# Two attention blocks and a mixture of experts on one core: first maxima, one transfer a row, expert weights by slices, lists in pieces

## The reference

```python
# block 1, per image, xf: [128, 1024]
f = softmax((theta_w @ xf).T @ (phi_w @ xf) / 8)        # 64 embedded channels
x = x + proj_w @ (f @ xf.T).T
t = tokens of x                                          # [4, 1024, 128]
# block 2
z = layernorm(t)
t = t + softmax((z Wq + bq)(z Wk + bk).T / sqrt(128)) (z Wv + bv)
# block 3: each token goes to 2 of 8 experts
z = layernorm(t)
top_w, top_i = top_k(z Wg + bg, 2);  w = softmax(top_w)
t = t + sum over both of w * (gelu(z W1[e] + b1[e]) W2[e] + b2[e])   # hidden size 512
```

## Time and profile before

| | us |
|---|---|
| median of three runs | 489.34 |
| the profiled execution | 489.35 |
| its span | 487.6 |
| TensorE busy | 389.0 (80%) |
| DVE busy | 370.3 (76%) |
| ACT busy | 335.2 (69%) |
| POOL busy | 313.0 (64%) |

### The profile page before, as it was taken

The page is one execution under the profiler, slowest core; times in us unless marked ns, Lnnn a source line. Parts: engine busy times, 40 slices in busy tenths (PEclk is TensorE's granted clock), DMA queues, the critical chain, the costliest instruction groups (busy, mean ns, idle before and its releaser), DMA issues.

```text
span 487.6 us, 12633 instructions
## 1 busy us (share of the span) xinstructions
PE 389.0 (80%) x3948; PEld 291.9 (60%) x3949; DVE 370.3 (76%) x1012; ACT 335.2 (69%) x636; POOL 313.0 (64%) x309
## 2 busy tenths in 40 slices
PE   2666669999988799989987876658989999999552
PEld 1433337666665466666655644646879898989321
DVE  2577989998897787889898588667976666666863
ACT  3635887778785499876756875558778787888320
POOL 9200132755699856598857857767777777777780
PEclk9988999999998999999999989778999999999955
DMA  6750000610000000000510101133355333334717
GB/s 216 169 93 0 1 0 3 151 25 3 1 1 0 2 1 1 1 1 2 137 38 12 31 27 40 51 88 94 91 127 132 105 101 93 98 94 113 225 49 258
DMA packets 43836, 32.62 MB, mean 67 GB/s; under 512 B 17686, under 2 KB 36905, under 8 KB 43785
## 3 DMA queue, kind: packets, MB, share of 16 engines
q1 hardware_dynamic: 39242, 22.59, 19.0%
q0 software_dynamic: 4544, 9.38, 5.8%
HBM read 18.33 MB, written 13.60 MB: 65 GB/s over the span
## 4 chain that ended last, share of the span: by engine, by line
PE 41%; DVE 31%; ACT 10%; issue 8%; POOL 6%; DMA 2%; SPq 1%; ACTq 0%; POOLq 0%; DVEq 0%
PE MX L696 13%; PE PV L696 11%; PE SC L696 11%; DVE mx L1519 6%; DVE EL L1542 5%; PE PR L696 4%; POOL ybuf L685 3%; ACT EH L1168 2%; ACT E L1167 2%; ACT QK L1076 2%; DVE QK L1493 2%; DVE EH L1738 1%; ACT X L1076 1%; PE PR L965 1%; DVE TOK L1561 1%
## 5 line engine op out<-in xcount | busy, mean ns | idle before, releaser
L1167 ACT ACTIVATE E<-SC 128x512 f32<-128x512 f32 x128 | 77.2, 603 | 43.4 <-PE SC L696 36.5
L696 PE MATMUL PV<-VH,EH 128*128 128x129 f16 x512 | 96.0, 227 | 3.0 <-DVE TOK L1561 3.0
L696 PE MATMUL SC<-QK 128*128 128x512 f16 x320 | 90.6, 389 | 8.2 <-ACT EH L1168 6.1
L618 POOL TENSOR_TENSOR EL<-E,EH 128x1024 f32 (+1 forms) x28 | 59.6, 2128 | 56.7 <-ACT EH L1168 56.7
L696 PE MATMUL PV<-VH,EL 128*128 128x129 f16 x512 | 95.6, 225 | 0.0
L696 PE MATMUL PV<-VL,EH 128*128 128x128 f16 x512 | 95.6, 223 | 0.0
L1519 DVE TENSOR_REDUCE mx<-MX 128x1 f32<-128x1024 f32 x64 | 78.0, 1219 | 18.8 <-PE MX L696 18.5
L685 POOL DMA_INDIRECT ybuf<-EL,yid x62 | 70.0, 1130 | 18.9 <-issue 17.4
L569 POOL DMA_INDIRECT zbuf<-ZZ,posi x64 | 66.4, 1038 | 21.3 <-issue 18.2
L1168 ACT ACTIVATE EH<-SC 128x512 f32 (+1 forms) x128 | 77.6, 606 | 0.0
L696 PE MATMUL MX<-QK,EH 128*128 x624 | 62.2, 246 | 1.9 <-DVE EL L1749 1.9
(11 more groups left out here) (231 smaller groups left out, 886.8 us busy)
## 6 DMA issues: line engine op xcount, KB each, us to landing
EH<-zbuf SPq DMA_DIRECT2D x39, 130.0 KB, 2.4
X<-in_x_dram SPq DMA_DIRECT2D x4, 512.0 KB, 5.1
zbuf<-zer SPq DMA_DIRECT2D x16, 128.0 KB, 4.0
X<-in_L_ffn_W_dram SPq DMA_DIRECT2D x1, 2048.0 KB
EL<-ybuf SPq DMA_DIRECT2D x4, 512.0 KB, 4.2
out_dram<-X SPq DMA_DIRECT2D x8, 256.0 KB, 4.8
W1H<-in_L_ffn_W_dram SPq DMA_DIRECT2D x4, 256.0 KB
W1L<-in_L_ffn_W_dram SPq DMA_DIRECT2D x4, 256.0 KB
```

Of the source, the lines that this page charges most:

```text
L618: nc.gpsimd.tensor_tensor(EL[:, w % 2, ds(i * 2, 2), c], E32h[1], EH[:, w % 2, ds(i * 2, 2), c], ALU.subtract).then_inc(e32_free[1], 1)
L696: return nc.tensor.matmul(o, w, r, start=start, stop=stop)
L1167: nc.scalar.activation(E32h[h][:, p, :], SC[:, p, :], ACT.Exp, scale=sc)
```

## The change

1. **Head.** ACT makes X16h before it copies TOK. Unit 0's eight maxima come ahead of unit 1's projections in step -1, through two PSUM tiles in turn (`first_maxima`: SC and MX), and the residuals of units 1 and 2 are transposed through half of PV. POOL makes X16l of unit 1. Step 0 is written out by hand: unit 0's scores begin after half of its row, the first low halves of its exponentials are POOL's (`e_low_first`), and unit 1's first two score groups stand in its last block.
2. **One transfer a row.** The 128x4 tile of maxima goes out in one transfer, which writes the row in the order token, tile; so the maxima's weights are read from QH with a step of four columns (`queries_apart`).
3. **SP's order.** The first rows of W1 are sent for after row 0, the zeros of the unused rows after row 1.
4. **Expert weights.** The clearings are in step 1, the four subtractions in steps 2, 2, 3 and 4; ACT makes one high slice in a pair, in steps 3 to 5, without the scaled copy; DVE makes the low slice from the unscaled one.
5. **Scatters.** Unit 0's tiles are scattered in other groups, unit 1's partly between the splits.
6. **Lists.** They are cut into pieces that are spread over pairs and expert tiles; the first one is made behind unit 7's last low half. Logits and rank of unit 2 come ahead of an output each. One register load instead of two.
7. **Mix.** For the first three units ACT scales the second results and DVE adds four tiles in one operation; the last unit is mixed as before.

```diff
@@ SP
-                for t in range(PAIRS):
-                    c = h * HALF + t * P
-                    sp.dma_start(QL[0:1, slot(m), c:c + P], mx16[:, h, t:t + 1]).then_inc(row_in[h], 16)
+                sp.dma_start(QL[0:1, slot(m), h * HALF:(h + 1) * HALF], mx16[:, h, :]).then_inc(row_in[h], 16)
...
                 row(m, 1)
+                if m == 0:
+                    expert_first_rows()
+                if m == 1:
+                    unused_tiles()
@@ tables
+        first_maxima = [(WIDE[0], MX[:])[t % 2 if t < 6 else 1] for t in range(T)]
+        OVER_MX = (0, B - 1)
+        ROWS_OF = {2: {0: 0, 2: 2}, 3: {1: 1}, 4: {0: 3}}
+        HIGHS_OF = {3: {0: 0}, 4: {0: 1, 2: 2}, 5: {1: 3}}
+        LOWS_OF = {3: {2: 0}, 4: {1: 1, 3: 2}, 5: {2: 3}}
@@ POOL
+                def e_low_first(i):
+
+                    pool.wait_ge(sc_free, (2 if isinstance(i, int) and i == 0 else first_half(i, 1)) + 2)
+                    c = slice(0, HALF)
+                    nc.gpsimd.tensor_tensor(EL[:, 0, ds(i * 2, 2), c], E32h[0], EH[:, 0, ds(i * 2, 2), c],
+                                            ALU.subtract).then_inc(e32_free[0], 1)
...
                             if i == PAIRS - 1:
                                 pool.wait_ge(rows_ready, 1)
-                                scatter(0, 2)
+                                scatter(0, IN_UNIT)
                             pair(i, (a, i - 1))
-                        scatter(2, 2)
+                        scatter(IN_UNIT, IN_UNIT)
...
-                    for i in range(PAIRS - 1):
-                        scatter(IN_UNIT * (i + 1), IN_UNIT)
-                        split_last(i)
-            for b in range(1, B):
+                    scatter(2 * IN_UNIT, IN_UNIT)
+                    split_last(0)
+                    scatter(3 * IN_UNIT, IN_UNIT)
+                    pool.wait_ge(rows_ready, 2)
+                    scatter(2 * T, IN_UNIT)
+                    split_last(1)
+                    scatter(2 * T + IN_UNIT, IN_UNIT)
+                    split_last(2)
+            scatter(2 * T + 2 * IN_UNIT, 2 * T - 2 * IN_UNIT)
+            for b in range(2, B):
@@ TensorE
+                def queries_apart(m, h):
+
+                    return QH[:, slot(m), h * HALF:(h + 1) * HALF].rearrange("k (q t) -> k t q", t=PAIRS)
...
+                    first_maximum(0)
+                    first_maximum(1)
+                    residual_half(1, 0)
+                    first_maximum(2)
+                    residual_half(1, 1)
+                    first_maximum(3)
+                    residual_half(2, 0)
+                    pe.wait_ge(x_lo, 2)
+                    products(1, 0)
+                    residual_half(2, 1)
+                    first_maximum(4)
+                    first_maximum(5)
+                    products(1, 1)
+                    continue
...
                     rows_whole()
-                    pair(1, False, second=True)
+                    outputs(1, 0)
                     logits_whole()
-                    pair(2, False, rest=True)
+                    outputs(1, 1)
+                    pe.wait_ge(e32_free[1], PAIRS * (a + 1) + 1)
+                    outputs(2, 0)
                     rank(2)
+                    outputs(2, 1)
                     pair(3, False, rest=True)
@@ ACT
-                    c = ds(i * S, S)
-                    cp(W1H[:, c], Xw[:, c], svec[:, 1:2])
-                    cp(Xw[:, c], Xw[:, c], svec[:, 1:2]).then_inc(wexp_scaled, 1)
+                    act.wait_ge(w1_augmented, HIGH_AFTER[i])
+                    c = slice(i * S, (i + 1) * S)
+                    cp(W1H[:, c], Xw[:, c], svec[:, 1:2]).then_inc(wexp_scaled, 1)
...
+            def second_results(k):
+
+                act.wait_ge(y_in[k], 16)
+                for t in range(PAIRS * k, PAIRS * (k + 1)):
+                    y = yin[t // T][:, t % T, 1, :]
+                    last = cp(y, y, WT[:, 1, t:t + 1])
+                last.then_inc(y_scaled, 1)
@@ DVE
+                def first_weights(i):
+                    dve.wait_ge(wexp_scaled, i + 1)
+                    dve.wait_ge(w1_augmented, LOW_AFTER[i])
+                    c = slice(i * S, (i + 1) * S)
+                    nc.vector.scalar_tensor_tensor(out=W1L[:, c], in0=Xw[:, c], scalar=svec[:, 1:2], in1=W1H[:, c],
+                                                   op0=ALU.mult, op1=ALU.subtract).then_inc(wexp_lo, 1)
...
+                    for t in range(PAIRS):
+                        first_maximum(t)
+                    scaled(0)
+                    lows(0)
+                    first_maximum(4)
+                    first_maximum(5)
+                    lows(1)
+                    first_maximum(6)
+                    values(2)
+                    first_maximum(7)
+                    scaled(1)
...
+            def mix_half(k):
+
+                dve.wait_ge(y_in[k], 16)
+                t = slice(PAIRS * k, PAIRS * (k + 1))
+                for i in range(PAIRS * k, PAIRS * (k + 1)):
+                    last = first_result(i)
+                link(last)
+                dve.wait_ge(y_scaled, k + 1)
+                at = slice(k % 2 * PAIRS, (k % 2 + 1) * PAIRS)
+                nc.vector.tensor_tensor(TOK[:, t, :], TOK[:, t, :], yin[k // 2][:, at, 1, :], ALU.add) \
+                    .then_inc(summed, PAIRS)
+                dve.wait_ge(summed, PAIRS * (k + 1))
```

More of the change, by code:

```diff
@@ L839, in rows_whole @@
                         for t in range(h * PAIRS, (h + 1) * PAIRS):
+                            if t == T - 2 and ahead_of_last is not None:
+                                ahead_of_last()
                             if t % 2 == 0:
@@ L881, in pair @@
                         transposes(3 * i)
-                    if u is not None:
+                    if u is not None and not ahead:
                         scores(u, i, 1, 0)
@@ L1282, in _ @@
+                pair(0, before, True)
+                if s in HIGHS_OF:
+                    for i in range(1, PAIRS):
+                        pair(i, (a, i - 1))
+                    continue
+                with act.Fori(1, PAIRS) as i:
                     pair(i, None if a is None else (a, i - 1))
```

427 lines of the change are left out of this document (304 added, 123 removed).

## The result

The changed kernel takes 468.88 us (median of four runs, 468.19 to 469.82) against 489.31 for the kernel before on the same chip: ratio 0.9584, 95% interval 0.9565 to 0.9603. The forecast was 463.4 with a range of 454 to 476. The profiled execution took 469.82, its span 468.0.

| stage | before | after | gain | forecast |
|---|---|---|---|---|
| to unit 0's second scale | 41.82 | 32.80 | 9.0 | 8.5 |
| step 0 | 28.1 | 27.5 | 0.6 | 2 |
| steps 1 to 5 | 161.8 | 155.2 | 6.6 | 4.5 |
| step 6 | 33.2 | 34.2 | -1.0 | 0 |
| unit 7's last scale to the first mix | 194.0 | 198.0 | -4.0 | 3 |

The account below looks back on a forecast made before the run. No engine was taken to bound the whole span (TensorE busy 80%; POOL the bound from 323.22 on). Gains of 10.5 (head), 4.5 (units), 3.0 (turn) and 8.0 (end) sum to 26.0: span 461.6, time 463.4 us, range 454 to 476.

Parts of the forecast that it names:

- The head: Start of the kernel: projections 3.1 us earlier, unit 0's second scale 8.5 earlier; with the next step 10.5.
- The units: Units 1 to 5: moving the expert weights' preparation off POOL shortens the steps, +4.5 us, bounds 0 and 8.
- bound of 8: Upper bound of the gain in units 1 to 5, if the three long steps all fall to 29.9 us.
- The end: DVE's last mixes: sharing them with ACT stops one put being held 10.0 us; +8.0, bounds 0 and +10.
- Step 0: The step after unit 0's second scale: less DVE and ACT work shrinks 28.1 us to some 26, gain 2.
- the expert stage at 0: Expert tiles: TensorE comes 4.8 us earlier, but POOL's scatters and puts set the end; term 0, bound -2.
- The turn: From attention to experts: lists, logits and rank reordered, unit 2's routing earlier, less extra scatters; +3.0, bounds 0 and 6.0.
- Rival B: Order on POOL eats the gain: extra scatters cost 6 and DVE's added operations fill the units; 469.9 us, chance 0.14.
- units 1: Second premise of Rival B: units gain only 1 us instead of 4.5, as DVE's added operations fill them.
- One transfer a row at 0: Eight transfers a unit become two: hidden in steady steps; term 0, between -1 and +2 over the units.
- Rival C: The maxima's strided weight loads take four times 98 ns, adding 37 us on TensorE: 500 us, chance 0.03.
- Rival D: Head's gain given back as unit 1's projections lengthen the next step, leaving 3.1 us: 470.8 us, chance 0.08.

Follow-up runs that it names:

- e6: The changed kernel with ACT copying unit 0's transposed residual ahead of the input's high half, as before: 472.12 us, ratio 0.9632.
- e3: The changed kernel with the mixes as before, on DVE alone and back to back for all units: 479.28 us, ratio 0.9774.
- e1: The changed kernel with TensorE's expert registers loaded in two loads (2 and 8) as before, instead of one of 10: 464.39 us, ratio 0.9472.
- e7: The changed kernel with TensorE's expert registers loaded in two loads of 4, two tiles ahead of first use, none carried: 463.87 us, ratio 0.9454.
- e4: The changed kernel with four transfers for each half row and contiguous queries as the maxima's weights: 482.03 us, ratio 0.9831.
- e8: The changed kernel with one of POOL's expert weight subtractions moved from step 2 to step 3: 469.55 us, ratio 0.9594.
- e2: The changed kernel with POOL's scatters in the old groups, unit 1's all behind the splits: 467.96 us, ratio 0.9539.
- e5: The kernel before with only the one transfer a half row and the strided queries it needs: 490.25 us against 489.42, ratio 1.002.

## Why the prediction was right, and where not

**Right in sign and size, and in part by luck in how the size is made up.** Three of its terms are in the traces. The head: 3.0 for ACT's order (e6: 3.1 at the second scale), the second scale at 32.8 (33.3). The units: ACT's wait of 5.82 is gone, and steps 3 to 5 fell; here the size was 2 us too small, since all three fell to 30 or 31, near the 29.9 of the step before. The prediction's bound of 8 for that case was summed wrong: from 33.4, 34.3 and 33.1 to 29.9 it is 11.1 for the three, and 10.4 with its other two steps. The end: one put had been held for 10 us, the new mix ends that, and e3 brings it back. I took 8 with bounds 0 and 10; the stage gave 8.4.

**Step 0** gave 0.6 and not 2. DVE fell to 19.26 as worked out (19.8), but ACT had 23.54 and not 20, and POOL got 16.23 (12.9 by the prediction's own numbers; the two clearings, 1.8 each, came in as well). That ACT's share would shrink because exponentials start earlier was wrong: two pairs of instructions start ahead of 32.80, at 28.18 and 29.45, not four, and two of unit 1 come in at the end, so the step has 14 pairs as before.

**The failed step: the expert stage at 0.** The prediction gave TensorE 4.8 us and said that they wouldn't count, because POOL's row of puts is the end. From unit 7's last scale to the first mix it became 4.0 slower, outside even the sum of the prediction's lower bounds for the turn and this stage (0 and -2); the four waits behind the load of 10 registers are 5.3 on the slow side. The edit was named in the description of the change, and no term stood for it: I had no row for a register load, and it should have been bounded by the row where one stood, which was the 0.4 to 0.9 that TensorE lost at each eighth tile before. Its cost also moved the bound: with it POOL waits for TensorE. Without it (e1, e7) POOL's row runs without waits again, as forecast, but it is the limit only in e7, and by 0.70; in e1 DVE's mixes begin behind TensorE's last tile and never wait for a put, so the two are level. The time is 464 then, within 1 us of the 463.4, and 4.5 of the gap of 5.5 us are this one edit.

That e1 comes so near is luck in part. By the prediction's stages its span of 461.9 gains 9.9 in the head (8.5 forecast), 0.5 in step 0 (2), 7.4 in steps 1 to 5 (4.5), -0.9 in step 6 (0), 0.4 from unit 7's last scale to the first mix (3) and 8.3 at the end (8): what the turn didn't bring, the units did.

**The turn** isn't shown. In the changed kernel's trace the scatter of unit 2 came 2.7 us earlier relative to unit 7's last scale (55.6 instead of 58.3), where 3.0 were forecast. But in the six other runs with the same turn that can be set beside it, it stands at 58.0 (e1, e3), 58.1 (e4), 56.9 (e8) and 59.5 (e6, e7), so one pair of traces can't carry a gain of 3. The granted clock of the stretch differs with it, 0.94 in the changed kernel, 0.91 in e1, e3 and e4, 0.85 in e8, 0.83 and 0.80 in e6 and e7, 0.88 before, though not in step with the time. No run takes the lists' or the logits' new places back, so what they bring stays open. Rival B's first premise, that the extra scatters eat the turn, is only half answered: with the old groups, at the same clock, the scatter stands where it stood (e2), but it might be up to 2 us in the time. Its second, units 1, fell.

**One transfer a row at 0** was right for the steady steps (e5) and hid the main thing: the new head is only a gain with it. In the prediction the wait for it was "inside the head's sum", with no number. Its number with four transfers is 14.3 us of TensorE's waits, with one 1.7. Had the change come without that edit, the end of step 0 would have been 12 us later than it was (72.67 against 60.32).

**Rival C, the strided loads.** They take 116 to 119 ns instead of 97 to 99. It needed 0.20 us more a load to decide, and got 0.02. The Trainium skill (SBUF — State Buffer, "Door 1: The DMA port swizzle") has this stride as free; the traces have some 20 ns a load against the kernel before, 13 and 21 against e4, and the time shows it no more than e5's interval allows.

**Rival D** was half there: step 0 kept its length, but the scale's 9.0 us stayed.

**The hold of a put.** The Trainium skill (SBUF — State Buffer, "SBUF: two separate sides") has whichever of DVE and GpSimd starts first keep the port pair for one whole instruction, while the other is blocked. Both traces with long rows of operations show one put held for a whole row (10.97 and 11.25 us) and released 0.83 to 0.85 us after its end; with the row broken each 1.9 us the longest put is 1.23. So the blocking agrees and its length doesn't; that it is this port pair no run shows.

## What to carry to other kernels

Price every edit of a change, those on a sequencer (register loads, branches) too, by the idle time that stands where one is now. A transfer that is hidden in steady steps is on the path as soon as its consumer is moved up to its producer, so cost the two edits together, not one by one. Where two engines are level at the end, a cost that looks free on one moves the bound to it.
